# VectorE's sample step, MLP-out step and last step of a block as two ranked steps each

## The reference, cut to what matters

```python
xp = x @ w_in + b_in
h = gelu(batchnorm(depthwise_conv3x3(x)))
offset, mask = h @ w_off + b_off, softmax(h @ w_msk + b_msk)
# per token, 4 groups x 9 taps: bilinear samples (4 corners) of xp, weighted by the mask, summed
y = dcn_core(xp, offset, mask) @ w_out + b_out
x = x + gamma1 * layer_norm(y, ln1_g, ln1_b)
m = gelu(x @ w_fc1 + b_fc1) @ w_fc2 + b_fc2
x = x + gamma2 * layer_norm(m, ln2_g, ln2_b)
n = ln(x)                                    # attention: query i sees all keys j < i
e = exp(w2 . tanh(n_i @ W1[:h] + n_j @ W1[h:] + b1) + b2)
t = x + (e @ n) / (sum(e) + 1e-10)
t = t + ffn(ln(t))                           # top-8 tokens of each of 64 experts
```

## Time and profile before

| | |
|---|---|
| median of 3 runs | 15138.87 us (15132.04 to 15160.17) |
| profiled execution: its own time / its span | 15154.41 us / 15152.6 us |
| busy PE / weight loads / DVE | 7392.2 / 3712.8 / 6055.5 us |
| busy ACT / POOL | 6766.0 / 6690.9 us |
| granted TensorE clock, mean | 0.702 |

### The profile page before, as it was taken

How to read it: one execution, slowest core, us unless ns; L and a number is a source line. 1 busy time by engine, 2 the same in 40 slices (tenths; PEclk the granted TensorE clock), 3 DMA queues, 4 the chain that set the end, 5 groups by cost and what they waited for, 6 DMA issues and landing times.

```text
span 15152.6 us, 152058 instructions
## 1 busy us (share of the span) xinstructions
PE 7392.2 (49%) x45113; PEld 3712.8 (25%) x45113; DVE 6055.5 (40%) x17780; ACT 6766.0 (45%) x8210; POOL 6690.9 (44%) x7060
## 2 busy tenths in 40 slices
PE   3345553445534555345444455444554445544557
PEld 1222222222222222122222222222222222222234
DVE  4443334433443334344344433434334434354343
ACT  1245642455424554245533455334553346533454
POOL 4444444444444444444444444444444444444430
PEclk6667776677766777677766677667776677766778
DMA  2111111111111111111111111111111111212325
GB/s 63 52 44 35 34 40 48 43 32 35 42 46 41 32 38 43 45 40 32 39 41 45 39 33 39 42 47 38 33 37 43 48 37 32 58 55 70 95 63 161
DMA packets 453936, 712.02 MB, mean 47 GB/s; under 512 B 146576, under 2 KB 261136, under 8 KB 451472
## 3 DMA queue, kind: packets, MB, share of 16 engines
q0 software_dynamic: 225792, 462.87, 11.6%
q1 hardware_dynamic: 227312, 239.24, 5.0%
HBM read 595.58 MB, written 105.96 MB: 46 GB/s over the span
## 4 chain that ended last, share of the span: by engine, by line
another core or an unknown queue 37%; ACT 20%; PE 13%; issue 12%; DVE 12%; DVEq 5%; DMA 1%; SPq 0%; POOL 0%; ACTq 0%; POOLq 0%
ACT tanh L1678 17%; PE score_ps L1846 6%; DVEq L1208 4%; DVE pool_mem L1373 2%; DVE newton L1242 2%; PE value_ps L1875 2%; DVE rstd L1244 1%; PE side_ps L1778 1%; DVE bst L1249 1%; ACT L1664 1%; PE turn_ps L1747 1%; ACT expo L1688 1%; ACT L1688 1%; ACT hid L1664 1%
## 5 line engine op out<-in xcount | busy, mean ns | idle before, releaser
L1678 ACT ACTIVATE tanh<-key_rep,query 128x896 f32<-128x896 f32 (+7 forms) x6400 | 5557.8, 951 | 5014.7 <-remote 2819.6
L1189 POOL DMA_INDIRECT pool_mem<-patches_odd,pool_mem x3528 | 3346.8, 949 | 4037.8 <-DVE y L1376 3014.6
L1189 POOL DMA_INDIRECT pool_mem<-patches_even,pool_mem x3528 | 3344.0, 948 | 3988.4 <-DVE y L1376 2890.2
L1846 PE MATMUL score_ps<-tanh,score_w 128*32 128x512 f32 (+3 forms) x24320 | 3613.8, 639 | 2235.8 <-ACT tanh L1678 1285.3
L1846 PEld LDWEIGHTS score_ps<-tanh,score_w 128*32 128x32 f32 x24320 | 832.7, 125 | 4411.0 <-issue 2787.7
L1875 PE MATMUL value_ps<-values,expoT 128*128 128x129 f32 (+1 forms) x5200 | 1009.8, 345 | 341.9 <-issue 275.8
L1373 DVE TENSOR_TENSOR pool_mem<-pool_mem 128x384 f32<-128x384 f32 x2352 | 1135.8, 552 | 50.7 <-issue 49.1
L1376 DVE TENSOR_REDUCE y<-pool_mem 128x64 f32<-128x2304 f32 x392 | 1000.8, 2553 | 53.2 <-issue 24.7
L1875 PEld LDWEIGHTS value_ps<-values,expoT 128*128 128x128 f32 (+1 forms) x5200 | 891.6, 248 | 435.4 <-issue 350.3
L1747 PE MATMUL turn_ps<-ident,expo 128*128 128x128 f32 (+1 forms) x2632 | 564.1, 339 | 830.6 <-DVE expoT L1442 433.6
L1442 DVE COPY expoT<-turn_ps 128x512 f32<-128x512 f32 (+4 forms) x800 | 457.1, 572 | 1203.2 <-remote 843.6
(11 more groups left out here) (166 smaller groups left out, 6210.9 us busy)
## 6 DMA issues: line engine op xcount, KB each, us to landing
pool_mem<-in_weight SPq DMA_DIRECT2D x64, 1024.0 KB, 9.2
pool_mem<-patches_even,pool_mem POOLq DMA_INDIRECT x3528
pool_mem<-patches_odd,pool_mem POOLq DMA_INDIRECT x3528
patches_even<-pool_mem SPq DMA_DIRECT2D x104, 256.0 KB, 2.0
patches_odd<-pool_mem SPq DMA_DIRECT2D x104, 256.0 KB
pool_mem<-in_x SPq DMA_DIRECT2D x56, 224.0 KB
x_tok<-in_x SPq DMA_DIRECT2D x192, 64.0 KB
x_d<-x SPq DMA_DIRECT2D x192, 64.0 KB
```

Of the source, the lines that this page charges most:

```text
L1189: pool.indirect_dma_start(gathered[:, b, j * 4 * CG:(j + 1) * 4 * CG], None, patches_flat[int(odd)], bass.IndirectOffsetOnAxis(ap=index[:, ...
L1678: nc.scalar.activation(tanh[:, ui % TANH_SLOTS, :w], key_rep[:, lo:lo + w], ACT.Tanh, bias=query[:, col:col + 1]).then_inc(tanh_done.sem, 1)
L1846: last = mm(score_ps[32 * col:32 * col + 32, ci % 2, lo:hi], score_w[:, place], tanh[:, ui % TANH_SLOTS, lo:hi], start=place == 0, stop=pl ...
```

## The change

`sample` becomes `weigh` (wait for the gathers, six multiplications, drain) and `sample` (wait that `y`'s buffer is free, reduction). `mlp_out` keeps the part up to `x1`, and `norm` takes the moments of `x1`, the write to `values` and the wait for the previous image's use of that place (`quad_used`). `finish` keeps the part up to `x2` with `x2_ready`, and `norm2` takes the rest with the wait for the previous `ln2_turned`. Each half has a due time, a length and a list of needs of its own. No DVE instruction that computes is added, dropped or reshaped.

```diff
@@ -197,8 +197,8 @@
     ("pe", "turn"): .35, ("pe", "mix"): .9, ("pe", "turn_mid"): .35, ("pe", "hidden"): 1.9, ("pe", "mlp_out"): 1.4,
     ("pe", "turn_norm"): .35, ("pe", "keys"): .9, ("pe", "route"): .35, ("pe", "logits"): .45,
     ("dve", "image_in"): .7, ("dve", "project_in"): .7, ("dve", "patches"): .8, ("dve", "offsets"): 4.7, ("dve", "weights"): 3.0,
-    ("dve", "sample"): 6.0, ("dve", "turn"): .35, ("dve", "mix"): 3.9, ("dve", "turn_mid"): .35, ("dve", "mlp_out"): 7.1,
-    ("dve", "turn_norm"): .35, ("dve", "keys"): 1.1, ("dve", "mask"): .35, ("dve", "finish"): 3.9, ("dve", "route"): .4, ("dve", "logits"): .4,
+    ("dve", "weigh"): 3.2, ("dve", "sample"): 2.7, ("dve", "turn"): .35, ("dve", "mix"): 3.9, ("dve", "turn_mid"): .35, ("dve", "mlp_out"): 3.9, ("dve", "norm"): 3.2,
+    ("dve", "turn_norm"): .35, ("dve", "keys"): 1.1, ("dve", "mask"): .35, ("dve", "finish"): 1.1, ("dve", "norm2"): 2.9, ("dve", "route"): .4, ("dve", "logits"): .4,
     ("act", "conv"): .6, ("act", "offsets"): .3, ("act", "hidden"): 1.3,
     ("dve", "u_max"): 3.5, ("dve", "u_match"): 3.5, ("dve", "u_differ"): 4.2, ("act", "u_exp"): 2.9, ("dve", "u_mul"): 4.5,
     ("pe", "u_turn"): .9, ("dve", "u_turn"): .7, ("pe", "u_pool"): 2.0, ("dve", "u_pool"): .4,
@@ -250,12 +250,15 @@
         due["x_in", k] = k - .02
         begin, pace = k + CHAIN_BEGIN, 1
         due["sample", 2 * k] = k - SAMPLE_URGENT
+        due["weigh", 2 * k] = due["sample", 2 * k] - .02
         if 2 * k + 1 < NSUB:
             due["sample", 2 * k + 1] = k + .5 - SAMPLE_URGENT
+            due["weigh", 2 * k + 1] = due["sample", 2 * k + 1] - .02
         else:
             begin, pace = k + .46, .75
         for name, at in zip(CHAIN, CHAIN_AT):
             due[name, k] = begin + pace * at - CHAIN_URGENT
+        due["norm", k] = due["turn_norm", k] - .02
         begin = max(free, begin + READY)
         span = max(.4, (SHARE[0] * (k + 1) + SHARE[1]) / SHARE[2] * blk_rows(k) / P)
         units = [u for u in UNIT_INDEX if u[0] == k]
@@ -269,6 +272,7 @@
             due["mask", k] = end + .02
             for q in range(-(-len(tiles) // 4) + 1):
                 due["values", k, c, q] = end + .05 + .05 * q
+        due["norm2", k] = end + .25
         due["finish", k], due["route", k], due["logits", k] = end + .2, end + .3, end + .4
         free = begin + span
     return due
@@ -313,8 +317,8 @@
         out["pool", ("sample", t)] = [at(0, "dve", "offsets", t // BAND_SUBS), at(0, "sp", "patches", NPATCH - 1),
                                       at(0, "sp", "patches", NPATCH - 2),
                                       at(int(last < 0), "dve", "sample", last % NSUB)]
-        out["dve", ("sample", t)] = [at(0, "pool", "sample", t), at(0, "dve", "weights", t // BAND_SUBS),
-                                     before("pe", "turn", t // 2, NBLK, 2)]
+        out["dve", ("weigh", t)] = [at(0, "pool", "sample", t), at(0, "dve", "weights", t // BAND_SUBS)]
+        out["dve", ("sample", t)] = [at(0, "dve", "weigh", t), before("pe", "turn", t // 2, NBLK, 2)]
     for k in range(NBLK):
         last = (k, len(chunks_of(k)) - 1)
         end = at(0, "pe", "values", *last, -(-len(chunks_of(k)[-1]) // 4))
@@ -329,18 +333,19 @@
         out["pe", ("hidden", k)] = [at(0, "dve", "turn_mid", k)]
         out["act", ("hidden", k)] = [at(0, "pe", "hidden", k)]
         out["pe", ("mlp_out", k)] = [at(0, "act", "hidden", k)]
-        out["dve", ("mlp_out", k)] = [at(0, "pe", "mlp_out", k), at(int(k < X1_SLOTS), "dve", "finish", (k - X1_SLOTS) % NBLK),
-                                      at(1, "pe", "values", old, len(chunks_of(old)) - 1, -(-len(chunks_of(old)[-1]) // 4))]
-        out["pe", ("turn_norm", k)] = [at(0, "dve", "mlp_out", k)]
+        out["dve", ("mlp_out", k)] = [at(0, "pe", "mlp_out", k), at(int(k < X1_SLOTS), "dve", "finish", (k - X1_SLOTS) % NBLK)]
+        out["dve", ("norm", k)] = [at(0, "dve", "mlp_out", k),
+                                   at(1, "pe", "values", old, len(chunks_of(old)) - 1, -(-len(chunks_of(old)[-1]) // 4))]
+        out["pe", ("turn_norm", k)] = [at(0, "dve", "norm", k)]
         out["dve", ("turn_norm", k)] = [at(0, "pe", "turn_norm", k)]
         out["pe", ("keys", k)] = [at(0, "dve", "turn_norm", k)]
         out["dve", ("keys", k)] = [at(0, "pe", "keys", k),
                                    at(1, "act", "unit", old, len(chunks_of(old)) - 1, blk_rows(old) // ROWS8 - 1)]
         out["dve", ("mask", k)] = [at(0, "act", "exp", *last)]
-        out["dve", ("finish", k)] = [end, before("sp", "route", k, NBLK, 2), before("sp", "logits", k, NBLK, 2),
-                                     before("pe", "route", k, NBLK)]
-        out["sp", ("route", k)] = [at(0, "dve", "finish", k)]
-        out["pe", ("route", k)] = [at(0, "dve", "finish", k), before("pe", "logits", k, NBLK)]
+        out["dve", ("finish", k)] = [end, before("sp", "route", k, NBLK, 2), before("sp", "logits", k, NBLK, 2)]
+        out["dve", ("norm2", k)] = [at(0, "dve", "finish", k), before("pe", "route", k, NBLK)]
+        out["sp", ("route", k)] = [at(0, "dve", "norm2", k)]
+        out["pe", ("route", k)] = [at(0, "dve", "norm2", k), before("pe", "logits", k, NBLK)]
         out["dve", ("route", k)] = [at(0, "pe", "route", k)]
         out["pe", ("logits", k)] = [at(0, "dve", "route", k)]
         out["dve", ("logits", k)] = [at(0, "pe", "logits", k)]
@@ -1359,13 +1364,11 @@
                     settle()
                     if isinstance(n, int) and n == images - 1 and i == NBAND - 1:
                         v.sem_inc(front_over, 1)
-                elif what == "sample":
+                elif what == "weigh":
                     slot = gather_slot(i)
                     g, tt = divmod(i, BAND_SUBS)
                     each = 16 * SAMPLES
                     dve.wait_ge(gather_done[slot], n * (SLOT_USES[slot] * each) + (slot_use(i) + 1) * each)
-
-                    dve.wait_ge(y_turned.sem, y_turned.free(n, i // 2, 2))
                     product = gathered[:, slot].rearrange("p (j c k) -> p j c k", c=CG, k=4)
                     weight = corner_w[:, g, tt].rearrange("p (j k) -> p j k", k=4)
                     for lo in range(0, SAMPLES, PIECE):
@@ -1373,6 +1376,10 @@
                         v.tensor_tensor(part, part, weight[:, lo:lo + PIECE].unsqueeze(2)
                                         .to_broadcast([P, PIECE, CG, 4]), ALU.mult)
                     settle()
+                elif what == "sample":
+
+                    dve.wait_ge(y_turned.sem, y_turned.free(n, i // 2, 2))
+                    product = gathered[:, gather_slot(i)].rearrange("p (j c k) -> p j c k", c=CG, k=4)
                     v.tensor_reduce(y[:, i // 2 % 2, b].rearrange("p (g c) -> p g c", c=CG),
                                     product.rearrange("p (g t) c k -> p g c t k", g=2), AX_XY, ALU.add)\
                         .then_inc(sampled.sem, 1)
@@ -1396,11 +1403,13 @@
                 elif what == "mlp_out":
                     r = blk_rows(i)
                     wait(mlp_done, n, i)
-
-                    wait(quad_used, n, last_use(QUAD_INDEX, i))
                     add_norm(chain_ps[:r, :C], x1, mid[:r], 3, r)
                     v.scalar_tensor_tensor(x1[:r, x1_place(odd, i)], ln_a[:r], rstd[:r], ln_b[:r], ALU.mult, ALU.add)
                     settle()
+                elif what == "norm":
+                    r = blk_rows(i)
+
+                    wait(quad_used, n, last_use(QUAD_INDEX, i))
                     moments(x1[:r, x1_place(odd, i)], r)
                     v.tensor_scalar(values[:r, value_place(odd, i), :C], x1[:r, x1_place(odd, i)], mv[:r, 0:1], rstd[:r], ALU.subtract, ALU.mult)\
                         .then_inc(norm_ready.sem, 1)
@@ -1449,8 +1458,6 @@
                     wait(quad_used, n, QUAD_INDEX[i, len(chunks_of(i)) - 1, -(-len(chunks_of(i)[-1]) // 4) - 1])
 
                     dve.wait_ge(block_out[b].sem, block_out[b].after(n, i // 2 - 1))
-
-                    wait(ln2_turned, n, i - 1)
                     v.tensor_scalar(den[:r, 0:1], value_ps[:r, C:C + 1], 1e-10, None, ALU.add)
                     settle()
                     v.reciprocal(den[:r, 1:2], den[:r, 0:1])
@@ -1458,6 +1465,10 @@
                     v.scalar_tensor_tensor(x2[:r, b], value_ps[:r, :C], den[:r, 1:2], x1[:r, x1_place(odd, i)],
                                            ALU.mult, ALU.add)
                     settle().then_inc(x2_ready.sem, 1)
+                elif what == "norm2":
+                    r = blk_rows(i)
+
+                    wait(ln2_turned, n, i - 1)
                     moments(x2[:r, b], r)
                     v.tensor_scalar(xln2[:r, b], x2[:r, b], mv[:r, 0:1], rstd[:r], ALU.subtract, ALU.mult)\
                         .then_inc(ln2_ready.sem, 1)
```

## The result

| | before | changed |
|---|---|---|
| time, median (lowest to highest) | 15143.46 us (15132.04 to 15160.17, 4 runs) | 15627.15 us (15624.25 to 15659.54, 4 runs) |
| ratio | | 1.0328, 95% interval 1.0312 to 1.0343 |
| profiled execution's span, granted clock | 15152.6 us, 0.702 | 15625.3 us, 0.693 |

The change makes the kernel 3.3% slower. I forecast 15350, 1.4% slower; the sign is right and the time lies in the range, but the loss is 484 us where I had worked out 210.

What follows compares the result with a forecast made beforehand. It took DVE's fixed order ahead of each reduction to set POOL's gaps. Per image 23.1 + 14.0 + 2.1 - 13.0 = +26.2 us, +210 for eight images, gave 15350 us, 1.4% slower; 8-in-10 range 14780 to 15850.

Steps and rivals of the forecast that it cites:

- What bounds the kernel: POOL's gaps end when DVE's fixed order reaches the next reduction; DVE's PE-dependent steps move only around gaps, about 9 us into bursts.
- paid in full: Whatever DVE does ahead of a reduction in a gap lengthens the time by its whole length; work in a burst's dead part is free.
- The signs in the trace: If right: POOL waits over 5904.7 us, even gaps 22 to 30 us, keys within 5 us, more 0.3 us bursts, period about 1872.
- the light pairs: Some 7 of 14 odd stretches with no `mlp_out` or `finish` and few PE waits, so the odd reduction falls into its burst.
- I take +2.0: Odd samples whose reduction falls into the burst: +2.0 us each at 7 places an image, bounds -2.5 and +6.8.
- +3.3: `mlp_out` and `norm` ahead of the even reduction, odd sample still behind its burst: +3.3 us at 7 places, bounds -5.4 and +6.2.
- Gathers: Multiplications running beside gathers at 7 places slow them by 0.3 us a sample, 2.1 us an image; full blocking would add 146 us.
- The waits at zero: A few semaphore waits checked at another place, for buffers long past where a half now waits: 0 us.
- The credit for `finish`: Splitting `finish` lets another step start earlier at 13 of 25 blocks: -13 us an image, bounds 0 and -40.
- Much slower: Rival, chance 0.13: light stretches do not get through in the live 9 us, all 14 pairs cost 6.2 us; 15830 us.
- Gaps pay for themselves: Rival, faster, chance 0.33: longer even gaps let ACT and PE get ahead, odd gaps shrink by 7.1 us; 14910 us.
- The order drawn anew: Rival, unchanged, chance 0.08: every engine's order changes, gains and losses may cancel the sum; time stays at 15139 us.

Runs made afterwards that it cites:

- reduce_late: Kernel before with each reduction moved behind `mlp_out` and `norm` where these came right behind it (16 samples an image): 16021.88 us, 1.0434 of before.
- weigh_early: Kernel before with a sample's six multiplications put right behind the previous sample's reduction, with some exceptions: 14982.92 us, 0.9759 of before.
- sample_again: Only the sample planned as two steps, `mlp_out` and `finish` whole, against the kernel before on chip 11: 15934.43 us, 1.0382 of before.
- landed_idle: Changed kernel plus a POOL pause behind every burst (wait until its gathers landed, three clears): 11292.51 us, 1.1974 of before, on a chip where before takes about 9430.
- waits_only: Changed code with all steps planned whole as before, so only the places of the waits differ: 9426.92 us, 1.0002 of before, on chip 12.

## Why the prediction was right or wrong

**What bounds the kernel, right.** DVE's queue ahead of a reduction sets the gaps on this kind of chip. `reduce_late` makes that queue longer and costs 4.3%; `weigh_early` makes it shorter and gains 2.4%, with no instruction that computes added or taken away in either. Only "paid in full" was too strong: 5.3 us were lost for 7.1 moved in, and 1.3 won for 2.9 moved out.

**The signs in the trace, right.** More waiting of POOL (6337.2 against 5904.7 us), even-triggered gaps of 26.9 instead of 17.8 us on average (25.48 and, above the 30 that I had named, 34.24 at the place shown), keys 0.73 us behind the burst's start at 7104.46 us (L1427 at 7105.19), and 7 more bursts an image at 0.3 us, the number that I had taken for the light pairs. In the second of the two there DVE did nothing. The period was wrong: 1908, not 1872.

**The step that failed: "I take +2.0", the price of an odd sample that falls into its burst.** It was the term that was mis-sized; the sum had 7 x 2.0 = 14 us an image for it, and the stretches around such samples took 70.7 us more, 8.8 for each of eight. I had read the price from pairs of an odd sample and the even one behind it. These pairs did cost what I said: nine odd samples (21, which did so before, and eight more) are now reduced 10 to 18 us on average behind the even one ahead of them, and each with the even one behind it they took 664.9 us an image before and 672.7 after (images 2 to 5), +0.9 for each. But the pair leaves out the even sample ahead, in whose stretch `mlp_out` and `norm` newly stand. At samples 4, 12, 16, 24 and 32, which are in none of these pairs, the intervals grew by 57.8 us, and the sum had no term for them. The trace before shows it once the sample ahead is taken in. Its reduction of sample 19, beside the earlier trace rows:

```profile
6328.17 2.55 DVE L1376 TENSOR_REDUCE y<-pool_mem 128x64 f32<-128x2304 f32 x1
```

Samples 20 to 22 took 6459.29 - 6328.17 = 131.1 us, and three average ones take 3 x 37.7 = 113.1: 18 us more, where the pair of 21 and 22 had shown 0.5 less than its average. I had seen in the earlier trace rows that the second of two bursts has no live part, and wrote that "nothing is gained but the gap itself"; its price had to be looked for on both sides of the pair, where the work that ACT and PE did not do in it has to be done.

**"+3.3" was too high.** I took it for blocks whose odd sample still ends behind its burst; the four such pairs in the table took 0.4 us more each in the first measurement, and about 3 on chip 11. The other 20 samples took 12.0 us less, close to the 13 that I gave to `finish`, but nothing ties it to that split.

**What the sum should have held.** A price for each burst that newly follows another, taken from what it loses: about the 9 us that were called live. With 54 such bursts that is 54 x 9 = 486 us, and 484 were measured. This near agreement is partly luck. Samples 12 and 14, which fell into bursts before, no longer do, and the five stretches scatter from 0.4 to 20.9 us. On chip 11 the same product gives 43 x 9 = 387 for the changed kernel (450 measured), 70 x 9 = 630 for `sample_again` (589), and 53 x 9 = 477 for `reduce_late` (677, so 200 us are missing). The counts there stand against the 43 of the first measurement's trace, as none of before was taken on chip 11. So the lost live time is the best reading of the traces, and the product comes out at 0.7 to 1.1 of what was measured; it is not a shown cause. Wherever an odd sample newly falls in, `mlp_out` and `norm` newly stand in the gap ahead of it too, so the trace can't part the two, and the kernel that would, `landed_idle`, never met such a chip. What is shown is that the late reduction costs, and that the longer gap alone cost little at the four blocks that had only that.

**The other terms.** Gathers: mean 952 ns against 948 and 949, 7056 x 0.0035 = 25 us in all, where I had 2.1 an image, 17 us; right. The Trainium skill (SBUF — State Buffer, "Who interferes with whom") infers that a tensor_tensor does not hold up descriptor generation. The traces agree for most gathers and not for all: in `weigh_early` 370 of 392 sets of multiplications run beside gathers, and the 782 gathers that meet a multiplication have a median of 1.10 us, where the others take 0.947 on average. But 30 of the 782 took 2.7 to 3.1 us. One of them, with the multiplications that it met:

```profile
7883.85 2.89 DVE L1393 TENSOR_TENSOR pool_mem<-pool_mem 128x384 f32<-128x384 f32 x6
7884.72 2.85 POOL L1211 DMA_INDIRECT pool_mem<-patches_even,pool_mem  x1 [36.57 <-DVE y L1400]
```

It ended 0.8 us behind the last of the six. So the block for the whole length, which I had set aside, does occur, and 30 x 1.9 = 57 of the 134 us that `weigh_early` pays are these. In the first measurement's trace of the changed kernel it is one gather of 7056, with 3.24 us. The waits at zero: `waits_only` took 1.0002 of before, but on the kind of chip on which no wait counts, so it stays argued. The credit for `finish`, 13 us an image, stays open, as said at `sample_again`.

**The rivals.** *Much slower* (15830) is nearer to the measured 15627 than my 15350 is, by 203 against 277 us, but not for its reason: it wanted light stretches that do not get through before the burst ends, and eight of them did get through. *Gaps pay for themselves* is refuted as a whole, since the period grew; one part of it came true, as more odd samples fell into their bursts than the seven of my sum, and that is where the loss lies. *The order drawn anew*, with an unchanged time, is refuted by the result; that the new order costs or gives something beside the late reductions is open.

## What to carry to other kernels

Where engines make progress only in part of the time, count that time over a whole period before and after, and price a lost stretch of it by the work it held; a local pair of rows shows the saved gap and hides what its neighbours on either side pay. Where one engine's queue releases another's long transfer, put ahead of the release only what must be there: moving 2.9 us of multiplications out of the gap gained 2.4%. And measure on more than one chip: on six of the seven chips whose number is known here the kernel before ran at about 9430 us, and on the one of these on which the changed kernel itself was run, the change was worth nothing, since another engine is the bound there.

## What was not expected of the hardware

The kernel takes 9424 to 9440 us on six chips and 15345 on a seventh, a factor of 1.6 for the same program. The difference is in the bursts: on the second kind PE works through them (10.52 of 13.60 us at the place shown), on the first it does much less behind the first 9 us of a burst (6.34 of 16.50 us) and in a second burst (4.01 of 22.30 above). POOL issued the gathers equally fast on both, with a median of 944 ns, as these rows of the changed kernel on chip 13 show beside the two above.

```profile
L1194 POOL DMA_INDIRECT pool_mem<-patches_even,pool_mem x883: 940/944/1319, 3437.3 to 5679.5; - x177
L1194 POOL DMA_INDIRECT pool_mem<-patches_odd,pool_mem x882: 940/944/1324, 3438.6 to 4558.9; - x177
```

The transfers were equally fast too. The queue of the gathers, packets, MB and share of the span, for the changed kernel in the first measurement and on chip 13:

```profile
q0 software_dynamic: 225792, 462.87, 11.2%
q0 software_dynamic: 225792, 462.87, 18.1%
```

That is 0.112 x 15625.3 = 1750 us and 0.181 x 9414.6 = 1704 us of each DMA engine's time, for the same packets. The cause was not found.
